# Attention over a graph: each head's row of shifts turned by VectorE and placed by four transfers, with the work around it moved

## The chip, the cores and the metric

The kernel runs on one core of a Trainium2 chip. The metric is the device time of one execution in microseconds (us); a comparison takes the median of several runs. The profile is of one execution. Its engines are TensorE (PE; PEld is its weight load), VectorE (DVE), ScalarE (ACT), GpSimd (POOL) and Sync (SP), whose queue issues all transfers here.

## The reference, cut to what matters

```python
h  = relu(layernorm(x))                              # 2048 x 256
hs = layer_norm(h, ln1);  ht = layer_norm(h_target, ln1)
q  = (ht @ Wq + bq) / sqrt(32); k = hs @ Wk + bk; v = hs @ Wv + bv     # 8 heads of 32
logits = where(adj != 0, q k^T, -1e30)               # 8 heads x 2048 targets x 2048 sources
ctx  = softmax(logits) @ v
ht = layer_norm(ht + ctx @ Wo + bo, ln2)
out = x + ht + gelu(ht @ W1) @ W2                    # W1 256 x 1024, W2 1024 x 256
```

`adj` is an int32 matrix of 2048 x 2048; `nodemask` masks nodes.

## The kernel before

**Tiling.** Targets go in four blocks (`NTB`) of 512. A block and a head make a unit `u` (32 in all, `k, r = divmod(u, 8)`: block `k`, place `r` in it). Each unit has 16 steps `s`, one per tile of 128 sources; `n = 16 u + s` numbers the tiles. Arithmetic is split into high and low 16-bit parts where precision asks for it.

**A softmax with a shift.** Exponentials need a shift per target, the negated maximum of its unmasked scores. It must be known before a unit's scores are made, so the scores are made twice. The "early" products (`early_scores`, 128 targets x 1024 sources, a "pair" `e`, 8 per unit) go into two PSUM buffers, where VectorE subtracts the mask and takes the maximum (`maxima`, L1123). These run ahead: in unit `u` at half-step `j` (two steps) the pair `8u + LEAD + j` is made, in `u0` two at a time at first (`pairs_at`). `RAMP = 8` pairs come ahead of the loop.

**How the shift reaches the scores.** ScalarE negates the four maxima columns (`negated`, L850) into column 96 of `shift` (128 x 4 x 97). TensorE multiplies the four slices by an identity (`shift_row`), which puts the shifts of the unit's 512 targets as row 96 into PSUM `aux`. ScalarE copies this row into row 96 of the queries `qT` (`row_out`, L855). Row 96 of `kT` holds ones, so the score product of 97 rows adds the shift. In a unit the negation stands at step 6, the products at step 8, the copy at step 9; the first score of the next unit is made at step 11, since scores run `AHEAD = 5` tiles ahead.

**A step.** TensorE: four mask products and one score product for tile `n + 5` (`scores`), half an early pair, now and then an auxiliary job, then the eight context products of tile `n` (`context`), which need the probabilities' low part. ScalarE: the exponential (L838). The low part, a subtraction of the bf16 high half, is VectorE's for the tiles in `DVE_LO` (L1131, four per unit) and GpSimd's for the others (L1333, twelve).

**Jobs between.** From block 1 on, units also hold what other blocks need: sums of the context's parts (`SUM_AT`, GpSimd), its normalising (`NORM_AT`, VectorE, L1150), its turning and output product (`CT_AT`, `WO_AT`), the next block's queries (`QT_AT`, `QP_AT`), the next masks (`MASK_DVE`, VectorE, L1111) and the loads of `adj` (`LOAD_AT`). Every order is written out by hand in each engine's queue. Sync's is in order too: in unit `r = 4` it issues twelve placements of the next block's queries (`place_q`), L350.

**The start.** After the projections, value products (`values(i)`, eight of them) leave PSUM as a high part (ScalarE, `high_values`) and a low one (VectorE, `low_values`, L1093). VectorE also adds up the features (`feature_sums`, L1098), from which TensorE makes a mean of the values (`mean_values`). Sync waits for `feat_done` before it loads W1 and W2 over the features, then places the last two groups of queries and keys, 30 placements, then loads `adj` for block 1.

**The tail.** Up products, gelu and down products by block. VectorE's `results(0)` come after the statistics of block 3 (`lead_stats`); the turning of the last context (`turn_context`) stands after the up products 5 and 6, the output rows (`out_row`) after 1 and 3.

## Time and profile before

| | |
|---|---|
| median of 3 runs | 711.27 us (708.77 to 711.74) |
| the profiled execution | 710.3 us, of which the span is 708.5 us |
| granted TensorE clock, mean | 0.995 of full speed |
| TensorE busy | 660.1 us |
| VectorE busy | 591.8 us |
| ScalarE busy | 455.1 us |
| GpSimd busy | 520.9 us |

A row in order of time gives start, duration, engine, line and operation, `out<-in`, shapes and a count; in brackets the idle time of the engine before it and what ended that. A busy time includes the pipeline's overlap for TensorE, so starts tell more than durations there.

### The profile page before, as it was taken

To read this page: it belongs to the slowest core of one execution; us is meant where nothing else is said; L and a number is where in the kernel's file an instruction comes from. 1 tells how busy PE (TensorE), PEld (TensorE's weight loads), DVE (VectorE), ACT (ScalarE), POOL (GpSimd) and SP (SyncE) were. 2 spreads that over 40 slices of the span, in tenths; PEclk is the share of its full clock that TensorE was granted. 3 is DMA by queue.
4 is the path that set the end of the run, shared out by engine and by line. 5 is a ranking of instruction groups with operands and counts; after the bars stand their busy time and mean duration, and the time that the engine had idled before them with its cause. 6 is when DMAs were issued, how large, how long until landed. Compare 5 with 4: busy or idle time off the path is not lost. (4 is left out here: it accounts for less than half of the span.)

```text
span 708.5 us, 20214 instructions
## 1 busy us (share of the span) xinstructions
PE 660.1 (93%) x8326; PEld 470.7 (66%) x8326; DVE 591.8 (84%) x972; ACT 455.1 (64%) x811; POOL 520.9 (74%) x495
## 2 busy tenths in 40 slices
PE   4996899999999999999999999999999899898998
PEld 4563566766776677667767766777677667456667
DVE  5996799989999989999999799989978897564661
ACT  4742566766776658677766686777666788756550
POOL 3620879889999966889999677999977777370430
PEclk9999999999999999999999999999999999999999
DMA  8735411113001020120001112021000000000001
GB/s 297 260 75 176 134 31 59 34 62 105 2 2 32 19 74 29 56 83 2 4 31 41 52 32 76 17 70 53 2 2 2 2 2 2 1 1 31 16 23 52
DMA packets 20795, 36.20 MB, mean 51 GB/s; under 512 B 2752, under 2 KB 13280, under 8 KB 20704
## 3 DMA queue, kind: packets, MB, share of 16 engines
q1 hardware_dynamic: 20704, 34.92, 15.8%
q8 instruction: 65, 1.06, 0.6%
q14 instruction: 26, 0.21, 0.1%
HBM read 26.49 MB, written 2.10 MB: 40 GB/s over the span
## 5 line engine op out<-in xcount | busy, mean ns | idle before, releaser
L1333 POOL TENSOR_TENSOR prob_lo<-prob 128x512 f16<-128x512 f32 x380 | 439.0, 1179 | 95.4 <-ACT prob L838 93.7
L838 ACT ACTIVATE prob<-score 128x512 f32<-128x512 f32 x512 | 305.0, 597 | 164.1 <-PE score L440 156.4
L440 PE MATMUL early<-kT,qT 96*128 96x512 f16 x512 | 192.2, 380 | 20.2 <-DVE half_max L1123 19.3
L440 PE MATMUL score<-nidentb,mask_nat 128*128 128x128 bf16 x2048 | 199.0, 220 | 2.9 <-ACT prob L838 1.6
L440 PE MATMUL score<-qT,kT 97*128 97x512 f16 x512 | 196.3, 383 | 0.0
L440 PEld LDWEIGHTS ctx<-v_sb,prob 128*128 128x128 bf16 x2048 | 159.1, 98 | 54.1 <-ACT raw L860 9.4
L440 PE MATMUL ctx<-v_sb,prob 128*128 128x65 f16 x2048 | 191.4, 193 | 0.6 <-POOL prob_lo L1333 0.5
L440 PE MATMUL ctx<-v_sb,prob_lo 128*128 128x65 f16 x2048 | 190.4, 193 | 0.0
L1123 DVE CUSTOM_DVE_ANT_0 early<-early,mask_nat,half_max 128x1024 f32<-128x1024 f32 x128 | 163.5, 1284 | 24.5 <-PE early L440 24.0
L1123 DVE CUSTOM_DVE_ANT_0 early<-early,mask_nat 128x1024 f32<-128x1024 f32 x128 | 156.8, 1228 | 23.2 <-PE early L440 21.2
L440 PEld LDWEIGHTS ctx<-v_sb,prob_lo 128*128 128x128 f16 x2048 | 142.7, 97 | 49.9 <-issue 4.0
L1131 DVE TENSOR_TENSOR prob_lo<-prob 128x512 f16<-128x512 f32 x132 | 132.9, 1008 | 4.1 <-ACT prob L838 4.0
L440 PEld LDWEIGHTS score<-nidentb,mask_nat 128*128 128x128 bf16 x2048 | 122.3, 98 | 6.8 <-ACT prob L838 3.7
L440 PEld LDWEIGHTS early<-kT,qT 96*128 96x128 f16 x512 | 50.3, 99 | 40.7 <-DVE half_max L1123 38.2
L1424 POOL TENSOR_TENSOR mask_nat<-mask_nat,tgt 128x256 f32<-128x256 f32 x16 | 15.3, 968 | 50.1 <-DVE mask_nat L1282 50.1
L440 PEld LDWEIGHTS score<-qT,kT 97*128 97x128 f16 x512 | 50.3, 98 | 0.0
L440 PE MATMUL early<-w_f,kT 128*128 128x256 f16 x384 | 42.8, 273 | 3.7 <-DVE adj_in L1292 3.7
L1268 DVE TENSOR_TENSOR kT<-qT,kT 128x512 f16<-128x512 f32 x32 | 27.0, 852 | 22.8 <-ACT kT L997 22.8
L440 PEld LDWEIGHTS early<-w_f,kT 128*128 128x128 f16 x384 | 37.4, 98 | 9.2 <-DVE adj_in L1292 4.2
L993 ACT ACTIVATE qT<-score 128x512 f32<-128x512 f32 x32 | 19.0, 593 | 25.3 <-PE score L440 22.0
L1123 DVE DVE_READ_ACCUMULATOR2_ANT half_max<- 128x1 f32 x256 | 35.2, 138 | 0.0
L1111 DVE TENSOR_SCALAR mask_nat<-adj_in 128x1024 bf16<-128x1024 int32 x26 | 29.9, 1153 | 0.0
(162 smaller groups left out, 597.2 us busy)
## 6 DMA issues: line engine op xcount, KB each, us to landing
adj_in<-in_adj SPq DMA_DIRECT2D x26, 512.0 KB, 3.9
qT<-q_stage SPq DMA_DIRECT2D x48, 64.0 KB, 2.0
kT<-mask_nat SPq DMA_DIRECT2D x48, 64.0 KB, 2.0
raw<-in_x SPq DMA_DIRECT2D x4, 512.0 KB, 5.6
tgt<-in_L_gnn_h_target SPq DMA_DIRECT2D x4, 512.0 KB, 11.4
prob<-in_adj SPq DMA_DIRECT2D x4, 512.0 KB, 10.2
nT<-in_L_gnn_W SPq DMA_DIRECT2D x2, 1024.0 KB, 6.8
mask_nat<-in_x SPq DMA_DIRECT2D x1, 2048.0 KB, 9.0
```

What stands on the lines that cost most here:

```text
L440: return nc.tensor.matmul(dst, w, m, start=start, stop=stop, **more)
L838: nc.scalar.activation(prob[:, n % SLOTS, :], score[n % 2][:, :], ACT.Exp).then_inc(exp_done, 1)
L993: nc.scalar.activation(gelu[:, f % 2, :], up[f % 2][:, :], ACT.Gelu_apprx_tanh).then_inc(gelu_ready, 1)
L1111: nc.vector.tensor_scalar(mask_half(k, i), adj_home(k, i), 0.0, BIG, ALU.is_equal, ALU.mult).then_inc(mask_dve, 1)
L1123: nc.vector.tensor_tensor_reduce(out=early[e % 2][:, :], in0=early[e % 2][:, :], in1=mask_nat[:, k % 2, t, half * HALF:(half + 1) * HALF], ...
L1131: nc.vector.tensor_tensor(prob_lo[:, n % SLOTS, :], prob[:, n % SLOTS, :], prob_hi(n % SLOTS), ALU.subtract).then_inc(lo_sem["dve"], 1)
L1268: nc.vector.tensor_tensor(g_lo[:, k % 2, f, :], gelu[:, f % 2, :], g_hi[:, k % 2, f, :], ALU.subtract).then_inc(g_lo_done, 1)
L1333: nc.gpsimd.tensor_tensor(prob_lo[:, n % SLOTS, :], prob[:, n % SLOTS, :], prob_hi(n % SLOTS), ALU.subtract).then_inc(lo_sem["pool"], 1)
L1424: nc.gpsimd.tensor_tensor(xin[:, n - 1, :], xin[:, n - 1, :], tgt[:, n - 1, :], ALU.add).then_inc(r_done, 1)
```

## The change

1. `negated` writes into columns 0 to 3 of `shift`, now 128 x 2 x 32. VectorE turns its 32 x 32 blocks (`turn_shifts`) into `shift_t`, where row `t` of each of the four blocks holds 32 shifts. Sync issues four transfers per unit (`place_shifts`), one per 128 targets, four pieces of 32 elements each, straight into row 96 of `qT`. The four products, the identity `ident16` and ScalarE's copy go.
2. The negation moves to step 3 (step 6 in `u0`), the turn stands on VectorE at half-step 2, ahead of its pair. `LEAD` becomes 16; `FILL = 4` more pairs come ahead of the loop, and `u0` has 12 pairs.
3. Moved: places of masks, adjacency loads (now before or after the unit's four transfers), sums, normalising, `CT_AT` and `WO_AT`. Every unit with `r = 5` gives VectorE three low parts in place of four, `u0` two in place of none.
4. At the start the low parts of value products 3 to 7 are GpSimd's, from an SBUF copy that ScalarE makes; the features are added up by six folds on GpSimd and one reduction on VectorE; the mean of the values follows the first five scores. `features(4)` and `high_parts(3)` move ahead on ScalarE, `target_stats(2)` behind on VectorE.
5. In the tail `turn_context` stands after the up products 5 and 7, `out_row` after 2 and 4, and the first two results between the statistics.

```diff
-LEAD = 14
+LEAD = 16
+FILL = 4
+V_DVE = 3
-SHIFT_STEP = 8
-CT_AT = {(2, 1): 0, (2, 4): 1}
-WO_AT = {(2, 11): 0, (3, 1): 1}
+SHIFT_AT, TURN_AT = 3, 2
+CT_AT = {(2, 6): 0, (2, 11): 1}
+WO_AT = {(2, 13): 0, (3, 1): 1}
-MASK_DVE = [(0, 6), (2, 1), (2, 4), (2, 7), (3, 7), (4, 3), (4, 7), (5, 3)]
-LOAD_AT = [0, 0, 0, 2, 2, 3, 4, 4]
-SUM_AT = [(0, 3), (0, 11), (1, 1), (1, 7)]
-NORM_AT = [(0, 5), (1, 1), (1, 3), (1, 5)]
+MASK_DVE = [(0, 6), (2, 4), (2, 6), (3, 2), (3, 7), (4, 3), (4, 7), (5, 3)]
+LOAD_AT = [(0, 0), (0, 0), (0, 1), (2, 1), (2, 1), (3, 1), (3, 1), (4, 1)]
+SUM_AT = [(0, 3), (0, 11), (1, 5), (2, 1)]
+NORM_AT = [(0, 5), (1, 1), (1, 5), (2, 2)]
-DVE_LO = [()] + [(2, 6, 10, 14)] * (UNITS - 3) + [tuple(range(1, STEPS, 2))] * 2
+DVE_LO = [(10, 14)] + [(4, 9, 14) if u % H == 5 else (2, 6, 10, 14) for u in range(1, UNITS - 2)] + [tuple(range(1, STEPS, 2))] * 2
...
+                def place_shifts(u):
+                    sp.wait_ge(shift_turned, u + 1)
+                    for t in range(TT):
+                        sp.dma_start(q_block(u // H)[SHIFT_ROW:SHIFT_ROW + 1, u % H, t * P:(t + 1) * P],
+                                     shift_t[t::HD, u % 2, :]).then_inc(shift_in[u % 2], 16)
...
                 sp.wait_ge(v_ready, NT // 2)
                 sp.wait_ge(feat_done, 1)
+                place_shifts(0)
...
-                            if LOAD_AT[i] == r:
+                            if LOAD_AT[i] == (r, 0):
+                                load_adj(k + 1, i)
+                    if u + 1 < UNITS:
+                        place_shifts(u + 1)
+                    if k + 1 < NTB:
+                        for i in range(PAIRS):
+                            if LOAD_AT[i] == (r, 1):
                                 load_adj(k + 1, i)
...
-                        pe.wait_ge(aux_done, AUX["shift", u] + 1)
+                        pe.wait_ge(shift_in[u % 2], TT * 16 * (u // 2 + 1))
...
-                def shift_row(u):
-                    pe.wait_ge(shift_ready, u + 1)
...
-                    for t in range(TT):
-                        last = mm(aux[0:SHIFT_ROW + 1, t * P:(t + 1) * P], shift[:, t, :], ident16[:, :], True, True)
-                    last.then_inc(aux_ready, 1)
...
-                for e in range(TT, RAMP):
+                for e in range(TT, RAMP + FILL):
                     for i in range(2):
                         early_scores(e, i)
-                    if e == RAMP - 2:
-                        mean_values()
-                shift_row(0)
                 for n in range(AHEAD):
                     scores(n)
+                mean_values()
...
-                    nc.scalar.activation(shift[:, :, SHIFT_ROW], half_max[:, u % 2, 1, :], ACT.Copy, scale=-1.0).then_inc(
-                        shift_ready, 1)
-
-                def row_out(u):
-                    job_here("shift", u)
-                    nc.scalar.activation(q_block(u // H)[SHIFT_ROW:SHIFT_ROW + 1, u % H, :], aux[SHIFT_ROW:SHIFT_ROW + 1, :],
-                                         ACT.Copy).then_inc(aux_done, 1)
+                    nc.scalar.activation(shift[:, u % 2, 0:TT], half_max[:, u % 2, 1, :], ACT.Copy, scale=-1.0).then_inc(shift_ready, 1)
...
-                        job = aux_job(u, s + 2)
-                        if job == ("shift", u + 1):
+                        if s == SHIFT_AT + 3 * (u == 0) and u + 1 < UNITS:
                             negated(u + 1)
...
+                def turn_shifts(u):
+                    dve.wait_ge(shift_ready, u + 1)
+                    if u > 1:
+                        dve.wait_ge(shift_in[u % 2], TT * 16 * (u // 2))
+                    nc.vector.transpose(shift_t[:, u % 2, :], shift[:, u % 2, :]).then_inc(shift_turned, 1)
...
                 for e in range(TT, RAMP):
                     maxima(e)
+                turn_shifts(0)
+                maxima(RAMP)
+                dve.wait_ge(folded, 6)
+                nc.vector.tensor_reduce(feat_all[:, :], fold[:, 0, :, 0:TB // 8], AX, ALU.add).then_inc(feat_done, 1)
+                for e in range(RAMP + 1, RAMP + FILL):
+                    maxima(e)
...
+                        if j == TURN_AT and u + 1 < UNITS:
+                            turn_shifts(u + 1)
                         for e in pairs_at(u, j):
                             maxima(e)
...
+                def fold_features(i):
+                    if i < 2:
+                        pool.wait_ge(nT_masked, DC * (2 * i + 2))
...
+                        dst, a, b = fold[:, i, :, :], nT[:, 2 * i, :, :], nT[:, 2 * i + 1, :, :]
...
+                fold_features(0)
+                for i in range(V_DVE, NT // 2):
+                    low_values(i)
+                    fold_features(i - V_DVE + 1)
...
                 for t in range(TT):
+                    if t % 2 == 0:
+                        result(0, t // 2)
                     lead_stats(NTB - 1, t, t == TT - 1)
                 lead_scale(NTB - 1, lead_width(NTB - 1))
-                results(0)
+                for t in range(2, TT):
+                    result(0, t)
```

## Rows read from the trace of the kernel before

**Rows 1.** The page: busy time, share of the span and instructions of each engine.

```profile
PE 660.1 (93%) x8326; PEld 470.7 (66%) x8326; DVE 591.8 (84%) x972; ACT 455.1 (64%) x811; POOL 520.9 (74%) x495
```

**Rows 2.** Windows of u1, u5, u7, u9 (start:end): length, each engine's busy time, clock, DMA.

```profile
93.05:109.46 16.41, 15.08 (x233) 10.88 (x231) 14.75 (x23) 10.62 (x20) 13.86 (x14) 1.00 0.11 33
160.02:177.05 17.03, 15.57 (x233) 10.71 (x231) 17.03 (x23) 11.12 (x21) 15.74 (x14) 1.00 0.38 110
191.96:206.86 14.90, 14.90 (x233) 10.91 (x231) 13.52 (x21) 11.02 (x22) 14.90 (x14) 1.00 0.01 2
221.83:239.01 17.18, 15.48 (x233) 10.78 (x231) 17.18 (x25) 10.63 (x21) 17.18 (x17) 1.00 0.11 32
```

**Rows 3.** TensorE in u7, in order of time: mask products of three steps.

```profile
198.08 0.39 PE L440 MATMUL score<-nidentb,mask_nat 128*128 128x128 bf16 x4
...
198.98 0.39 PE L440 MATMUL score<-nidentb,mask_nat 128*128 128x128 bf16 x4
...
200.11 0.39 PE L440 MATMUL score<-nidentb,mask_nat 128*128 128x128 bf16 x4
```

**Rows 4.** Groups of instructions: busy us, mean ns of one, idle before.

```profile
L1131 DVE TENSOR_TENSOR prob_lo<-prob 128x512 f16<-128x512 f32 x132 | 132.9, 1008 | 4.1 <-ACT prob L838 4.0
...
L855 ACT ACTIVATE qT<-aux 1x512 f16<-1x512 f32 x32 | 18.9, 589 | 1.3 <-PE aux L440 0.5
...
L1150 DVE TENSOR_TENSOR q_stage<-raw,rden 128x256 f32<-128x256 f32 x16 | 13.2, 824 | 0.0
...
L440 PE MATMUL aux<-ident,shift 128*97 128x128 f16 x128 | 12.4, 218 | 2.0 <-ACT shift L850 2.0
```

**Rows 5.** The same view: VectorE's small operations.

```profile
L1170 DVE TENSOR_TENSOR col_l<-col_l,node_f 128x4 f32<-128x4 f32 x4 | 2.9, 723 | 0.1
...
L1169 DVE RECIPROCAL col_l<-col_l 128x4 f32<-128x4 f32 (+1 forms) x4 | 0.7, 180 | 0.4 <-ACT col_l L878 0.4
```

**Rows 6.** Sync's queue in order of time: issues of transfers, in three stretches.

```profile
2.32 0.33 SPq L371 DMA_DIRECT2D vec_r<-in_L_gnn_ln_scale  x1
...
4.44 0.25 SPq L371 DMA_DIRECT2D vec_r<-in_L_gnn_ln_bias  x1
...
60.57 0.90 SPq L409 DMA_DIRECT2D nT<-in_L_gnn_W  x2
...
81.90 1.08 SPq L345 DMA_DIRECT2D adj_in<-in_adj  x2
...
296.29 8.25 SPq L350 DMA_DIRECT2D qT<-q_stage  x12
```

**Rows 7.** Issues of transfers by tile: KB each, median us from issue to landing.

```profile
adj_in<-in_adj SPq DMA_DIRECT2D x26, 512.0 KB, 3.9
...
kT<-mask_nat SPq DMA_DIRECT2D x48, 64.0 KB, 2.0
...
kT<-ones SPq DMA_DIRECT2D x1, 32.0 KB, 10.4
```

**Rows 8.** The start in order of time: GpSimd's last masking, TensorE's products.

```profile
40.09 2.63 POOL L1357 TENSOR_TENSOR nT<-nT,qT 128x512 f32<-128x512 f32 x2 [3.58 <-ACT nT L784]
...
56.20 1.99 PE L440 MATMUL ctx<-cT,nT 128*128 128x256 f32 x8 [1.96 <-DVE v_sb L1093]
58.55 1.99 PE L440 MATMUL aux<-cT,nT 128*128 128x256 f32 x8 [0.35 <-DVE v_sb L1093]
...
68.18 0.48 PE L440 MATMUL score<-nidentb,mask_nat 128*128 128x128 bf16 x4 [0.68 <-ACT qT L855]
```

**Rows 9.** VectorE in u0 in order of time: the first maxima of two half-steps.

```profile
80.41 1.29 DVE L1123 CUSTOM_DVE_ANT_0 early<-early,mask_nat,half_max 128x1024 f32<-128x1024 f32 x1 [0.32 <-PE early L440]
...
83.28 1.29 DVE L1123 CUSTOM_DVE_ANT_0 early<-early,mask_nat,half_max 128x1024 f32<-128x1024 f32 x1 [0.32 <-PE early L440]
```

**Rows 10.** TensorE in the tail in order of time: its two longest waits.

```profile
617.30 0.63 PE L590 MATMUL aux<-ident,q_stage 128*128 128x128 f32 x4 [2.66 <-ACT cT L869]
...
646.38 5.41 PE L440 MATMUL early<-w_f,kT 128*128 128x256 f16 x48 [2.96 <-DVE adj_in L1292]
```

More of the change, by code:

```diff
@@ L81, in aux_job @@
     k, r = divmod(u, H)
-    if s == SHIFT_STEP + (u == 0):
-        return ("shift", u + 1) if u + 1 < UNITS else None
     if k + 1 < NTB and (r, s) in QT_AT:
@@ L102, in aux_numbers @@
 def aux_numbers():
-    jobs = [("shift", 0)] + [aux_job(u, s) for u in range(UNITS) for s in range(STEPS) if aux_job(u, s)]
+    jobs = [aux_job(u, s) for u in range(UNITS) for s in range(STEPS) if aux_job(u, s)]
     jobs += [("cT", NTB - 1, c) for c in range(DC)] + [("wo", NTB - 1, i) for i in range(TT // 2)]
@@ L116, in pairs_at @@
     if u == 0:
-        first = RAMP + (2 * j if j < 6 else j + 6)
-        return range(first, first + (2 if j < 6 else 1))
+        first = RAMP + FILL + (2 * j if j < 4 else j + 4)
+        return range(first, first + (2 if j < 4 else 1))
     first = u * PAIRS + LEAD + j
@@ L191, in gnn_kernel @@
         mean_v = sb("mean_v", [P, H, VS], F16)
-        shift = sb("shift", [P, TT, SHIFT_ROW + 1], F16)
+        shift = sb("shift", [P, 2, HD], F16)
+        shift_t = sb("shift_t", [P, 2, HD], F16)
         half_max = sb("half_max", [P, 2, 2, TT], F32)
@@ L310, in value_bank, with value_read @@
                 return early[1][:, i * TB:(i + 1) * TB]
-            return (score if i < 4 else (ctx, aux))[i % 2][:, :]
+            return ((ctx, aux) if i in (4, 5) else score)[i % 2][:, :]
+        def value_read(eng, i):
+            if i < V_DVE:
+                eng.wait_ge(v_lo, i + 1)
+            else:
+                eng.wait_ge(v_out, i - V_DVE + 1)
         def raw_of(k):
@@ L529, in scores @@
                     if n < 2:
[L531 removed]
+                        value_read(pe, n + 6)
                     else:
@@ L1209, in _ @@
                 low_values(0)
-                for k in range(1, 3):
-                    target_stats(k)
+                target_stats(1)
                 low_parts(2)
+                target_stats(2)
                 low_values(1)
@@ L1283, in shifted_rows, with result @@
                                                        in1=xin[:, n, :], op0=ALU.mult, op1=ALU.add).then_inc(t1_done, 1)
+                def result(k, t):
+                    n = k * TT + t
+                    dve.wait_ge(r_done, n + 1)
+                    dve.wait_ge(down_ready, n + 1)
+                    if n >= 4:
+                        dve.wait_ge(stored[n % 4], n // 4 * 16)
+                    nc.vector.scalar_tensor_tensor(out=yout[:, n % 4, :], in0=row[n % 2], scalar=node_f[:, n:n + 1],
+                                                   in1=xin[:, n, :], op0=ALU.mult, op1=ALU.add).then_inc(y_done, 1)
                 def results(k):
                     for t in range(TT):
[L1287 to L1293 removed]
+                        result(k, t)
                 denominators(NTB - 1)
@@ L1358, in drop_sources, with low_values @@
                                                 ALU.mult).then_inc(nT_masked, 1)
+                def fold_features(i):
+                    if i < 2:
+                        pool.wait_ge(nT_masked, DC * (2 * i + 2))
+                        if i == 0:
+                            pool.wait_ge(tp_ready, DC * len(GROUPS))
+                        dst, a, b = fold[:, i, :, :], nT[:, 2 * i, :, :], nT[:, 2 * i + 1, :, :]
+                    else:
+                        pool.wait_ge(folded, i)
+                        half = TB >> (i - 2)
+                        dst, a, b = fold[:, 0, :, 0:half], fold[:, 0, :, 0:half], fold[:, 0, :, half:2 * half] if i > 2 else fold[:, 1, :, :]
+                    nc.gpsimd.tensor_tensor(dst, a, b, ALU.add).then_inc(folded, 1)
+                def low_values(i):
+                    pool.wait_ge(v_hi, i + 1)
+                    full = v_full[:, i % 2, :].rearrange("p (t h d) -> p t h d", t=2, h=H)
+                    tiles = slice(2 * i, 2 * i + 2)
+                    nc.gpsimd.tensor_tensor(v_sb[:, tiles, :, HD:2 * HD], full, v_sb[:, tiles, :, 0:HD], ALU.subtract).then_inc(v_lo_pool, 1)
                 def context_sum(k, t):
@@ L1372, in _ @@
                 nc.gpsimd.memset(dead_w[:, :], DEAD_W).then_inc(made, 1)
-                for m in (ident32, identb, nidentb, ident16):
+                for m in (ident32, identb, nidentb):
                     last = nc.gpsimd.memset(m[:, :], 0.0)
                 link(last)
-                for m, one in ((identb, 1.0), (ident32, 1.0), (nidentb, -1.0), (ident16, 1.0)):
+                for m, one in ((identb, 1.0), (ident32, 1.0), (nidentb, -1.0)):
                     last = nc.gpsimd.affine_select(out=m[:, :], in_=m[:, :], compare_op=ALU.not_equal, fill=one, base=0,
```

78 lines of the change are left out of this document (29 added, 49 removed).

## The prediction

> **What bounds the kernel now.** The order of reading: the page's engine row, the windows by head unit, the order in time of TensorE inside one unit, the waits of the slow units, then the start and the tail. A "unit" is one head of one block of 512 targets; there are 32, u0 to u31, of 16 steps each. TensorE is busy 93% of the span and VectorE 84% [rows 1], but the mean hides two kinds of unit. In u7 TensorE has no idle time in 14.90 us, while VectorE is busy 13.52: TensorE bounds it. In u5 VectorE is busy in all of the 17.03 us and TensorE in 15.57; in u9 VectorE and GpSimd are busy in all of the 17.18 us and TensorE in 15.48 [rows 2]. u13 and u21 look like u5; u17 and u25 like u9. ScalarE is never above 0.75 of such a window. So a TensorE instruction taken out is worth its time in most units, in these six only a VectorE instruction is.
>
> **The products that go.** In u7 the starts of two mask products one step apart are 198.08 and 198.98: a step is 0.90 us. The step that also holds the four shift products is 198.98 to 200.11, 1.13 us [rows 3]. The mean of 218 ns of each product [rows 4] is mostly pipeline overlap; what leaves the queue is 0.225 us for four. It counts in the units that TensorE bounds: u2 to u30 without the six, 23 units, **-5.2 us**. ScalarE's copy of the row, 589 ns [rows 4], I count at nothing: ScalarE is busy 11.02 of 14.90 us in u7 [rows 2], and that idle time hides it; without that cover it would be worth 0.6 us a unit.
>
> **The turn and the transfers that come.** No row shows VectorE turning a block. It moves 32 columns of 128 rows. The nearest rows are of 128x4: a reciprocal at 180 ns, and a two-input operation at 723 ns [rows 5], whose like can be as short when nothing holds it. I take 0.2 us, near the first, because it too has one input; the ends are 0.1 and 0.7. In u7 VectorE has 1.4 us to spare, so even 0.7 is hidden there; in the six it is on the path.
> The four transfers: the smallest issues of the trace, eight of two rows each, start 0.30 us apart (2.32 to 4.44, seven steps); an issue of 32 rows takes 0.6 to 0.7 (12 in 8.25 us) [rows 6]. I take 0.30 each, since a shift transfer has four tiny pieces: 1.2 us in all, at most 2.7. From issue to landing the placements take 2.0 us; the ones, a one-partition transfer issued behind loads, took 10.4 [rows 7]. Is that early enough? The maxima now run two pairs further ahead (LEAD 16), so those of unit u+1 are done when unit u begins. ScalarE negates after its fourth exponential of unit u; VectorE turns after its second pair there. In u7 the step of 198.98 is step 8, so the unit starts at 198.98 - 8 x 0.905 = 191.7; the second pair's products end with step 3, at 195.3, its maximum 1.3 us later [rows 9], at 196.6. Plus 0.2, 1.2 and 2.0 makes 200.0. The first score of the next unit is issued at step 11, 191.7 + 11 x 0.905 = 201.7. So 1.7 us of slack: hidden, **0**. Everything behind that score on TensorE (context products, and through them ScalarE, GpSimd) would stop if it were late.
> Sync's queue is in order. At the end of r=4 it issues 12 placements of queries in 8.25 us [rows 6], for u12 until 304.54, and the new transfers of u13 come behind: 305.8, landing 307.8, while step 11 of u13 is at about 307.3. That is 0.3 us late on the mean of u5, u13, u21. They in turn lose one of four residual subtractions on VectorE (1008 ns [rows 4]; with it GpSimd has 15.74 + 1.2 us of work in u5 [rows 2], some 0.7 more than the unit would last, which the five steps by which scores run ahead absorb) and gain the turn: -1.0 + 0.2 + 0.3, three times: **-1.5 us**. u9, u17, u25 lose one normalising product of VectorE (824 ns [rows 4]) and a sum on GpSimd to r=2, where TensorE bounds: -0.82 + 0.2, three times: **-1.9 us**. The other moved masks and adjacency loads stay within the units' VectorE cover and come before the loads of the same step: 0; without cover each would cost about what a subtraction does, 1.0 us.
> u30 no longer has the last two pairs (early products): four products of 512 columns, each as many columns as the four shift products together, 0.22 us: **-0.9 us**.
>
> **The start.** At 56.20 and 58.55 TensorE waits 1.96 and 0.35 us for VectorE's residuals of v [rows 8]. These go to GpSimd behind a ScalarE copy, and the feature sums too, so the remaining four pairs of u0 begin at about 58 instead of 58.55 + 1.8 = 60.4, and are done near 63. But the shifts of u0 are placed only after Sync's wait for feat_done, and that now hangs on GpSimd: from 43 on, six folds and five residuals. Two instructions of 512 elements took 2.63 us [rows 8], so 1.2 to 1.3 each. The first fold is free; the first residual waits for the fourth value product and two ScalarE copies, until about 50. From there five residuals (6 us) and folds of 1024, 1024, 512, 256 and 128 elements (7 us), with a tenth for collisions and 0.3 for the reduction: I get 64.8 for feat_done, 66.0 for the last issue, 68.0 for landing. The first score was at 68.18 [rows 8]: nothing is gained, and the mean products, now behind the first five scores, put 0.9 us on TensorE less what they cover: context starts **+0.4 us**. (Four more pairs are hidden in this gap.)
> u0 has 12 pairs in place of 14; two pairs take VectorE 2.87 us (80.41 to 83.28), 0.32 of it waiting [rows 9]. Two steps with one pair cost 1.8, so this is -2.1. But the turn for u1 stands before VectorE's fifth pair, and waits for a negation placed behind ScalarE's exponential of step 6, which needs TensorE's score of step 6: VectorE idles about 2.5 us. Then the row for u1 is late: Sync starts its 30 placements about 5.4 us later than before (feat_done 64.8 and 1.2 of issues against 60.57), so the two loads issued at 81.90 [rows 6] go out at 87.3, and the transfers last at 89.6, behind 1 MB that needs until about 92 (such a load lands in 3.9 us [rows 7], two in about 5). Step 11 of u0 would be at about 89.6: 2.5 us of stall. From this VectorE catches up, and u1's 1.3 us of TensorE idle (16.41 against 15.08 busy [rows 2]) go. Sum -2.1 + 2.5 + 2.5 - 1.3, and 1.4, two thirds of 2 x 1.0, for the two subtractions that u0 now gives VectorE: **+3.0 us**.
>
> **The tail.** At 646.38 TensorE idles 2.96 us for a result row held behind VectorE's statistics [rows 10]; results 0 and 1 now go between them: -2.9. At 617.30 it idles 2.66 us for ScalarE's cT [rows 10]; with an up product in front of it 1.2 of that is filled. **-4.1 us**.
>
> **Sum:** -5.2 - 1.5 - 1.9 - 0.9 + 0.4 + 3.0 - 4.1 = -10.2 us. The profiled execution took 710.3 us (708.5 of span, 1.8 around it), so 700.1; the median of the three runs is 1.0 above that one: **701 us**.
>
> **A rule to weigh.** The row first: the two-input operation on 128x4 takes 723 ns on the mean for 4 columns [rows 5], beside a GpSimd that is nearly always busy. The Trainium skill (SBUF — State Buffer, "SBUF: two separate sides") says why: VectorE operations with two SBUF inputs and GpSimd's share one pair of ports, whoever starts first has it for the whole instruction. By that rule moving folds and residuals to GpSimd can hold the masks of the start by one fold each (an estimate from that page and the rows: three times 1 us, which would make it 704), while the maxima, which read PSUM and one SBUF operand, go on. The sum above does without it.
>
> **Rivals.**
> 1. The row is late in every unit. For: the slack is 1.7 us, and no row shows so small a transfer between partitions. Against: placements of 64 KB land in 2.0. It costs from the point where turn, issues and landing exceed 201.7 - 196.6 = 5.1 us; with 0.62 us per issue and a landing of 3.9, it is 6.6: 1.5 late, 31 times, less the 10: 748; with half of that excess 724. Slower.
> 2. The start costs more: the transfers for u1 land as late after issue as the 10.4 us row, or the folds on GpSimd are held up (the rule's locks): about 6 us more, 707.
> 3. The turn costs 0.7 us: six units lose 0.5 each, 704.
> 4. The start costs nothing: VectorE does not idle at the turn, and the loads do not hold the row: 695.
>
> **Chances and range.** Forecast 0.54 (own range 697 to 704.5); rival 1 0.08; rival 2 0.15, about half of it still over 0.5% faster; rival 3 0.10; rival 4 0.13. 0.5% is 3.6 us, about what three runs of this kernel can tell from nothing. Faster 0.54 + 0.13 + 0.10 + 0.07 = 0.84; same 0.08; slower 0.08. Range 693 to 709: rival 4 with the turn at 0.1 below, rival 2 with its bound above; rival 1 stays outside.
>
> **What would show it.** Steps of u7 all at 0.90 and its window at 14.7; u5 near 16.1 and u9 near 16.6; a TensorE wait before the first score of u1 of some 2.5 us, named a DMA wait, and VectorE idle 2.5 us before the turn for u1; feat_done's reduction near 64.5; no TensorE idle of 3 us in the tail. I am wrong if TensorE waits for a transfer in unit after unit, or if the first score comes after 71.

## The result, and the profile after

| | median | runs | ratio to before, with its 95% interval |
|---|---|---|---|
| before | 710.1 us (708.77 to 711.74) | 6 | |
| changed | 715.0 us (714.19 to 717.78) | 6 | 1.0071 [1.0049, 1.0093] |

The changed kernel is 0.7% slower, 4.9 us. The forecast was 701.0 with a range of 693 to 709, so the sign was wrong too. The profiled execution took 714.19 us, its span is 712.4; before, 710.3 and 708.5. These 3.9 us of span are placed first. The page of the changed kernel, busy times:

```profile
PE 656.2 (92%) x8198; PEld 463.4 (65%) x8198; DVE 595.2 (84%) x993; ACT 438.6 (62%) x784; POOL 538.3 (76%) x506
```

TensorE has less to do (656.2 against 660.1 [rows 1]) and yet more time passes. Windows of the changed kernel, the same view as [rows 2]: u0 from its first score on, u1, u5, u7, u9 and u10; length, busy time of PE, PEld, DVE, ACT, POOL, then clock, DMA share, GB/s.

```profile
71.95:103.28 31.33, 24.33 (x266) 15.87 (x267) 18.22 (x33) 13.01 (x24) 17.12 (x17) 0.87 0.57 165
103.28:119.36 16.08, 14.75 (x229) 10.58 (x227) 14.76 (x23) 10.03 (x19) 14.10 (x14) 1.00 0.10 34
169.96:186.29 16.33, 14.89 (x229) 10.60 (x227) 15.82 (x24) 10.42 (x20) 15.71 (x14) 1.00 0.20 49
200.86:215.43 14.57, 14.57 (x229) 10.63 (x227) 14.21 (x23) 10.44 (x21) 14.57 (x14) 1.00 0.22 75
230.46:247.52 17.06, 14.93 (x229) 10.66 (x227) 17.06 (x27) 10.04 (x20) 16.91 (x16) 1.00 0.10 33
247.52:268.50 20.98, 19.12 (x255) 13.93 (x252) 18.66 (x34) 11.18 (x23) 17.70 (x18) 1.00 0.16 51
```

u7 lost 0.33 us, u5 0.70, u9 0.12. Before, u0 lasted 24.87 us from its first score (68.18 to 93.05) at a mean clock of 0.93; now it lasts 31.33 at 0.87. u10 lasts 20.98 us against 19.32. The whole, stretch by stretch (a unit ends where ScalarE copies its context):

| stretch | predicted | measured |
|---|---|---|
| up to the first score | +0.4 | +3.8 |
| u0 and u1 | +3.0 | +6.5 - 0.3 |
| the products, 22 units and u30's part | -5.2 | 19 of them -1.7; u10, u18, u26 +1.7, +1.6, +1.5 |
| u5, u13, u21 | -1.5 | -0.70, -0.85, -0.91 |
| u9, u17, u25 | -1.9 | -0.12, -0.13, -0.38 |
| u30's early products | -0.9 | -1.4, with its part of the products |
| tail (end of u30 to the end) | -4.1 | -4.6 |
| sum | -10.2 | +3.9 |

Of the 14 us between the sums, two places carry 11: the start (9.9 against 3.4) and the units r = 2 (4.7 against nothing). The rest is mostly the products.

**The start.** VectorE of the changed kernel, in order of time:

```profile
38.72 3.04 DVE L1117 TENSOR_SCALAR mask_nat<-adj_in 128x1024 bf16<-128x1024 int32 x2
41.68 3.43 DVE L1117 TENSOR_SCALAR mask_nat<-prob 128x1024 bf16<-128x1024 int32 x2
45.03 0.74 DVE L1096 SCALAR_TENSOR_TENSOR mask_nat<-ctx,cols,mask_nat 128x512 f16<-128x512 f32 x1
```

GpSimd in the same stretch:

```profile
38.10 2.71 POOL L1375 TENSOR_TENSOR nT<-nT,qT 128x512 f32<-128x512 f32 x2 [1.69 <-ACT nT L798]
...
41.17 2.78 POOL L1389 TENSOR_TENSOR raw<-nT 128x1024 f32<-128x1024 f32 x1
```

and TensorE:

```profile
45.92 3.62 PE L466 MATMUL ctx<-nT,cT 128*128 128x512 f32 x4 [2.73 <-DVE mask_nat L1096]
```

Before, the same two pairs of masks:

```profile
38.10 1.28 DVE L1111 TENSOR_SCALAR mask_nat<-adj_in 128x1024 bf16<-128x1024 int32 x2
39.30 1.29 DVE L1111 TENSOR_SCALAR mask_nat<-prob 128x1024 bf16<-128x1024 int32 x2
```

Now the first pair lies beside GpSimd's last masking and takes 3.04, and the second beside the first fold (L1389, whose result the third fold, at 60.18, is the first to read) and takes 3.43. The first mask of the second pair by itself, seen in a narrower window:

```profile
41.68 2.83 DVE L1117 TENSOR_SCALAR mask_nat<-prob 128x1024 bf16<-128x1024 int32 x1
```

It starts 0.5 us into the fold and ends at 44.51, 0.56 us after the fold's end (43.95); such a mask takes 0.69 us in the kernel before. The residuals behind the masks (L1096) are 3.7 us late, TensorE waits 2.73 us for them, and the key products that follow take 3.62 us (1.96 in experiments 1 and 4, below): the window 45.85 to 49.26 has a granted clock of 0.50, the lower of the two levels (1.2 GHz).

Sync's queue, in order of time:

```profile
68.64 2.23 SPq L369 DMA_DIRECT2D qT<-shift_t  x4
70.91 0.95 SPq L429 DMA_DIRECT2D nT<-in_L_gnn_W  x2
71.92 1.86 SPq L362 DMA_DIRECT2D qT<-q_stage  x3
73.82 8.46 SPq L362 DMA_DIRECT2D kT<-mask_nat  x12
82.32 1.92 SPq L362 DMA_DIRECT2D qT<-q_stage  x3
84.28 8.21 SPq L362 DMA_DIRECT2D kT<-mask_nat  x12
92.54 1.08 SPq L357 DMA_DIRECT2D adj_in<-in_adj  x2
93.66 2.22 SPq L369 DMA_DIRECT2D qT<-shift_t  x4
```

Four shift transfers take 2.2 us to issue (each 492 ns, 0.58 us from one start to the next), where 1.2 was predicted. The two adjacency loads go out at 92.54, where the prediction had 87.3, and the four transfers for u1 from 93.66 on. TensorE in u0 waits for both the turn and the row:

```profile
88.57 0.60 PE L466 MATMUL early<-kT,qT 96*128 96x512 f16 x2 [2.26 <-DVE half_max L1129]
...
98.43 0.40 PE L466 MATMUL score<-nidentb,mask_nat 128*128 128x128 bf16 x4 [2.81 <-DMA qT<-shift_t]
```

The turn at the same place on VectorE:

```profile
87.07 0.21 DVE L1140 STREAM_TRANSPOSE shift_t<-shift 128x32 f16<-128x32 f16 x1 [2.80 <-ACT shift L870]
```

The turn takes 0.21 us, as taken, and idles 2.80 us for the negation, as foreseen (2.5).

**Windows at the lower clock.** These three stretches of the changed kernel are found in its clock record (the column behind the busy times):

```profile
45.85:49.26 3.41, 3.34 (x4) 1.51 (x5) 2.92 (x5) 0.00 (x0) 0.00 (x0) 0.50 0.23 57
66.33:76.57 10.24, 7.73 (x32) 3.40 (x33) 5.68 (x12) 2.70 (x6) 4.64 (x6) 0.50 0.42 131
90.23:93.64 3.41, 3.41 (x33) 2.29 (x30) 2.50 (x5) 1.19 (x2) 1.04 (x1) 0.50 0.35 84
```

Together 17.1 us; the kernel before has two stretches of 3.4 us, one at its first scores and one in the tail (experiment 8). The first of the three comes at the end of the wait of 2.73 us, the third 1.7 us after that of 2.26. Ahead of the second TensorE waited 1.1, 0.6 and 0.6 us before three early pairs. The longest wait, 2.81 us at 98.43, was followed by none.

A wait doesn't settle whether a stretch follows. Experiment 4 has the start of the changed kernel unchanged, and the same wait:

```profile
45.85 1.96 PE L466 MATMUL ctx<-nT,cT 128*128 128x512 f32 x4 [2.67 <-DVE mask_nat L1096]
```

Here the four products take 1.96 us at full clock, no stretch is near, and the first score comes at 70.24, 1.7 us before the changed kernel's. So of the +3.8 at the first score, 2.1 are the late masks and 1.7 the half clock behind them.

Executions of one kernel differ mostly in their time at half clock. Of the kernel before, those at a mean clock of 0.998 have spans of 706.8 to 707.3 us, those at 0.995 708.4 to 708.8, those at 0.990 710.9 to 711.6 and those at 0.986 714.2 to 714.3. The changed kernel's three at 0.988 (712.4 to 712.7) lie between the last two: its loss comes together with more time at half clock, and at a like clock it is no slower than the kernel before. How much of that time waits hide, no run separates. So 1.7 us between two single profiles can be one stretch more or less.

**r = 2.** TensorE in u10, whose window is above:

```profile
255.56 0.66 PE L608 MATMUL aux<-ident,q_stage 128*128 128x128 f32 x4 [1.20 <-DVE q_stage L1163]
```

The turned context (`CT_AT`, step 6) waits for the normalising (L1163), which the change moved to the same unit; in u26 the same wait is 0.92 us, in u18 only 0.22. u10 and u18 also have one of 0.61 us for a low part of GpSimd. I had counted the units r = 2 as bound by TensorE and the moved work as free there.

### The profile page after: what moved, and what is told of

Read it like the earlier page. It is cut to its first block and busy times, and to the rows that moved or that the text cites. A ratio compares the mean times of both kernels' runs of the same rounds, so it can differ in the third digit from the quotient of the medians.

```text
span 712.4 us, 20092 instructions
## 1 busy us (share of the span) xinstructions
PE 656.2 (92%) x8198; PEld 463.4 (65%) x8198; DVE 595.2 (84%) x993; ACT 438.6 (62%) x784; POOL 538.3 (76%) x506
## 5 line engine op out<-in xcount | busy, mean ns | idle before, releaser
L1144 DVE TENSOR_TENSOR prob_lo<-prob 128x512 f16<-128x512 f32 x130 | 137.4, 1060 | 1.1 <-ACT prob L858 0.7
L1117 DVE TENSOR_SCALAR mask_nat<-adj_in 128x1024 bf16<-128x1024 int32 x26 | 27.2, 1050 | 0.0
```

The source lines that it names most:

```text
L1117: nc.vector.tensor_scalar(mask_half(k, i), adj_home(k, i), 0.0, BIG, ALU.is_equal, ALU.mult).then_inc(mask_dve, 1)
L1144: nc.vector.tensor_tensor(prob_lo[:, n % SLOTS, :], prob[:, n % SLOTS, :], prob_hi(n % SLOTS), ALU.subtract).then_inc(lo_sem["dve"], 1)
```

## The experiments

Each ratio is to runs of the kernel before on the same chip (medians 710.6). "Changed" is the kernel of the change; its median was 715.0, beside 710.1 for the kernel before.

**1. The first fold waits for the masks.** Changed, with one more wait on GpSimd:

```diff
@@ fold_features
                         if i == 0:
                             pool.wait_ge(tp_ready, DC * len(GROUPS))
+                            pool.wait_ge(mask_dve, TT)
```

> The changed kernel, with one wait more: GpSimd's first fold waits until VectorE has made its four first masks. Theory (collision): in the changed kernel these four masks take 6.4 us instead of 2.4, because the fold and they hold the same ports; TensorE then waits 2.7 us and runs 3.4 us at the half clock. With the wait the masks take 2.4 to 3.5 us, TensorE reaches the fourth key projection at about 43.2 instead of 45.9, there is no half-clock stretch there, the first score starts about 4 us earlier (68 instead of 72), and the time falls by 4 to 5 us, to about 710.5. Rival (the start is held by Sync and the transfers alone, the collision is absorbed): under 1 us of change.

Measured: 712.5 us (10 runs), ratio 1.0021 [0.9997, 1.0046], 2.5 less than changed. VectorE of this kernel:

```profile
38.70 3.05 DVE L1117 TENSOR_SCALAR mask_nat<-adj_in 128x1024 bf16<-128x1024 int32 x2
41.67 1.28 DVE L1117 TENSOR_SCALAR mask_nat<-prob 128x1024 bf16<-128x1024 int32 x2
42.87 0.74 DVE L1096 SCALAR_TENSOR_TENSOR mask_nat<-ctx,cols,mask_nat 128x512 f16<-128x512 f32 x1
```

The second pair is back at 1.28 us, the first still lies beside GpSimd's masking. TensorE in the same place:

```profile
43.75 1.96 PE L466 MATMUL ctx<-nT,cT 128*128 128x512 f32 x4 [0.58 <-DVE mask_nat L1096]
```

Its wait is 0.58 instead of 2.73, the clock stays up, and the first score is issued at 68.13 instead of 71.95. So one fold in the wrong place, with the stretch at half clock behind it, explains the whole +3.8 at the first score. The expectation of 4 to 5 us in all was nearly twice too high. The 3.9 us are still there at the end of u1; 2.0 go between u2 and u30, in u5, u13 and u21 (rows up to 0.4 us later) and in u17 and u18, where this execution has a stretch at half clock that the changed kernel's has not.

**2. The row of u1 ahead of the last placements.** Changed; Sync issues the transfers of u1 before the fourth head pair's placements:

```diff
                 for g in range(2, TT):
+                    if g == 3:
+                        place_shifts(1)
                     place_q(0, range(g, g + 1))
...
-                    if u + 1 < UNITS:
+                    if 0 < u < UNITS - 1:
                         place_shifts(u + 1)
```

> The changed kernel, with Sync's four transfers for u1 moved ahead of the last 15 placements and of the two loads of the next block. Theory (the row queues behind 30 placements and 1 MB): the wait of 2.8 us before u1's first score is gone and the time falls by 2.5 to 3 us, to about 712.3. Rival (the wait only hides another, the late turn on VectorE): under 1 us. Rival 2 (the 15 placements, now later, hold the first mask of block 1): no change or slower by up to 3 us.

Measured: 718.7 us, ratio 1.0125 [1.0101, 1.0148]. No TensorE wait for the row of u1 is left and u0 ends at 100.37 instead of 103.28, but u1 lasts 20.83 us instead of 16.08. A row of VectorE of this kernel:

```profile
104.53 0.69 DVE L1119 TENSOR_SCALAR mask_nat<-adj_in 128x1024 bf16<-128x1024 int32 x1 [3.99 <-DMA adj_in<-in_adj]
```

The wait went from the row to the adjacency of block 1, which now stands behind it in Sync's queue, and grew: TensorE waits 4.56 us there.

**3. u0's turn one pair later.** Changed, with `if j == TURN_AT + (u == 0)` for VectorE's turn.

> The changed kernel, with VectorE's turn for u1 one half-step later in u0 (after the fifth and sixth pair and not before them). Theory: VectorE's idle time of 2.8 us before the turn and TensorE's wait of 2.3 us behind it go, and the half-clock stretch at 90 us too, but the row still queues in Sync's queue, which is free only at 93.7: the wait before u1's first score grows by what is saved, and the time changes by less than 1 us. Rival (the turn's idle time is on the path): 2 to 4 us faster.

Measured: 716.8 us, ratio 1.0096 [1.0074, 1.0119]. VectorE's idle time at the turn is gone, and TensorE's wait for the row grew from 2.81 to 6.15 us; u0 ends at 105.17. The 1.8 us more than changed aren't clear of the scatter, since two of the changed kernel's six runs lie at 716.8 and 717.8. While Sync is the bottleneck, filling VectorE's gap gives nothing.

**4. The moved jobs back.** Changed, with the tables as in the kernel before:

```diff
-CT_AT = {(2, 6): 0, (2, 11): 1}
-WO_AT = {(2, 13): 0, (3, 1): 1}
-MASK_DVE = [(0, 6), (2, 4), (2, 6), (3, 2), (3, 7), (4, 3), (4, 7), (5, 3)]
-LOAD_AT = [(0, 0), (0, 0), (0, 1), (2, 1), (2, 1), (3, 1), (3, 1), (4, 1)]
-SUM_AT = [(0, 3), (0, 11), (1, 5), (2, 1)]
-NORM_AT = [(0, 5), (1, 1), (1, 5), (2, 2)]
+CT_AT = {(2, 1): 0, (2, 4): 1}
+WO_AT = {(2, 11): 0, (3, 1): 1}
+MASK_DVE = [(0, 6), (2, 1), (2, 4), (2, 7), (3, 7), (4, 3), (4, 7), (5, 3)]
+LOAD_AT = [(0, 0), (0, 0), (0, 1), (2, 1), (2, 1), (3, 0), (4, 0), (4, 1)]
+SUM_AT = [(0, 3), (0, 11), (1, 1), (1, 7)]
+NORM_AT = [(0, 5), (1, 1), (1, 3), (1, 5)]
```

> The changed kernel, with the places of the context's turning and output product, of masks, loads, sums and normalising inside the units as in the kernel before. Theory (the moved jobs cost what the removed products save): the units u10, u18, u26 (21.0, 20.0, 20.4 us in the changed kernel) fall by 1.5 to 2 us each and u11, u19 by 0.4, the time falls by 4 to 6 us, to about 710. Rival (VectorE's turn and the lead of the maxima cost it, wherever the jobs stand): these units stay within 0.5 us and the time within 1 us.

Measured: 710.4 us (10 runs), ratio 1.0003 [0.9988, 1.0018], 4.6 less than changed. Windows of u9 and u10 in this kernel:

```profile
227.72:245.54 17.82, 15.25 (x231) 10.53 (x228) 17.82 (x26) 10.01 (x19) 17.82 (x18) 1.00 0.10 31
245.54:264.79 19.25, 18.38 (x255) 14.01 (x252) 18.24 (x34) 11.15 (x22) 16.16 (x16) 1.00 0.17 57
```

The moved jobs relieve u9 by 0.76 us (17.06 against 17.82) and load u10 by 1.73 and u11 by 0.79. With them back, u10, u18 and u26 together are 0.5 under the kernel before, and the 19 units that the table counts apart 3.7 under it. (This profile is of the fastest of the ten executions.)

**5. Another order of Sync's start.** Changed; all 30 placements and both rows go ahead of the wait for the feature sums:

```diff
-                sp.wait_ge(v_ready, NT // 2)
-                sp.wait_ge(feat_done, 1)
                 place_shifts(0)
-                for i, (dst, w) in enumerate(((w1, W1), (w2, W2))):
...
                 for g in range(2, TT):
...
+                place_shifts(1)
+                sp.wait_ge(v_ready, NT // 2)
+                sp.wait_ge(feat_done, 1)
+                for i, (dst, w) in enumerate(((w1, W1), (w2, W2))):
...
-                    if u + 1 < UNITS:
+                    if 0 < u < UNITS - 1:
                         place_shifts(u + 1)
```

> The changed kernel with another order in Sync's queue at the start and nothing else: after the four shift transfers of u0 come the placements of the last two head pairs, then the shift transfers of u1, and only behind them the wait for the feature sums and the two weight loads; in the changed kernel the shifts of u0 waited for the feature sums and those of u1 stood behind 24 placements, four weight and adjacency loads. Theory (the row for u1 waits in Sync's queue, and the row for u0 for the feature sums): first score at 70.8 instead of 71.95, the DMA wait of 2.8 us before u1's first score gone, u0 ends near 99.5, and the kernel takes about 711. Rival (row_first showed it: what is moved ahead delays the next thing, now the weight loads or block 1's adjacency, and TensorE waits for VectorE's mask instead): u1 ends no earlier than in the changed kernel, 715.

Measured: 717.5 us, ratio 1.0086 [1.0056, 1.0117]. The rival held. (Against the 715.0 of changed the 2.5 us more are not clear of the scatter: the intervals overlap.) The first score comes at 70.49 and u0 ends at 99.42, both as the theory said, but u1 lasts 21.07 us: TensorE waits 4.21 us for the maxima and these for block 1's adjacency, as in experiment 2. Order alone can't mend a queue with more in it than time.

**6. Order, fold and jobs together.** Experiments 5, 1 and 4 in one kernel.

> The Sync order of sp_order, the first fold on GpSimd held until VectorE's four masks are done (fold_waits), and the places of the moved work in r=1 to r=4 as before (jobs_back), together. Theory: the three repairs lie in different stretches and add up: the order about -4, the fold -2.5, the places -4.5, from 715, makes 704. Rival: the start's repairs overlap, since each removes the lateness of the same first score and of the same row for u1, and all that they give together is what the larger gives: 707 or more.

Measured: 704.6 us, ratio 0.9915 [0.9885, 0.9945]. It was the size that the theory gave, though not by its terms: the order, counted at -4, gave nothing alone, and with the other two (-2.5 and -4.6) it gives the 3.3 that are left of the 10.4. The first score is at 66.97, u0 ends at 95.19, and u1 still lasts 20.51 us. VectorE of this kernel:

```profile
98.75 0.95 DVE L1118 TENSOR_SCALAR mask_nat<-adj_in 128x1024 bf16<-128x1024 int32 x1 [3.39 <-DMA adj_in<-in_adj]
```

**7. Only the shift path on the kernel before**, with the order of experiment 5 and u0's turn for u1 one pair later: turn, transfers, `LEAD = 16`, `FILL = 4`; sums, value parts, jobs and tail untouched.

> The kernel before with only the shift row changed: VectorE's turn and four transfers instead of the products and the copy, with 16 pairs of lead, and the Sync order of sp_order. The feature sums, the value residuals, the places of masks, loads, sums and normalisings, and the tail stay as in the kernel before. Theory (the shift path itself gains in the units that TensorE bounds, 0.33 us each in 23 units, 0.9 for u30, and costs 2 to 3 us in the start): 705. Rival (it is the shift path that costs; the moved work is innocent): not faster than before, 710 or more.

Measured: 719.4 us, ratio 1.0118 [1.0083, 1.0154]. The theory's 705 was wrong by 14 us. Sync begins the placements at 70.85 (the turn of u0 stands ahead of them), against 61.5 before, and u0 ends at 103.10, 10 us late; from u1's end to u30's it is 4.0 us shorter than before. The profile is of the slowest of the four (722.0), and 2.9 of its loss lie in the tail, where nothing was changed: it has stretches at half clock by the two long waits there, 10.2 us in all, against 3.4 in the kernel before.

**8. Only the tail's moves on the kernel before:**

```diff
-                    if f in (5, 6):
-                        turn_context(NTB - 1, f - 5)
+                    if f in (5, 7):
+                        turn_context(NTB - 1, f // 2 - 2)
...
-                    if f in (1, 3):
+                    if f in (2, 4):
...
                 for t in range(TT):
+                    if t % 2 == 0:
+                        result(0, t // 2)
                     lead_stats(NTB - 1, t, t == TT - 1)
...
```

> The kernel before with only the tail's moves: the second turned context one place later, the output rows one place later, the first two results of block 0 between VectorE's row statistics. Theory: TensorE's idle times of 2.66 and 2.96 us near 617 and 646 go, the kernel is 4 to 5 us faster than before, 706, and nothing changes ahead of the tail. Rival: the tail gains only because the changed kernel comes to it without the half-clock stretch, so that the moves alone give less than 2 us.

Measured: 705.5 us, ratio 0.9928 [0.9904, 0.9952], 5.1 less than before. Both long waits of [rows 10] are gone. What is left in TensorE's tail:

```profile
616.41 1.47 PE L440 MATMUL score<-nTq,w_f 128*128 128x512 f16 x6 [1.43 <-ACT qT L993]
619.00 4.06 PE L440 MATMUL score<-qT,w_f 128*128 128x512 f16 x18 [0.69 <-DVE qT L1176]
628.80 1.13 PE L440 MATMUL aux<-wo,cT 128*128 128x256 f32 x4 [0.54 <-ACT tgt L873]
```

Gone as well is a stretch at half clock that followed the wait at 617.30 in the kernel before; a window of that kernel:

```profile
617.90:621.30 3.40, 3.40 (x10) 1.22 (x8) 1.30 (x3) 1.73 (x4) 0.00 (x0) 0.50 0.00 0
```

But the stretch doesn't hang on the wait alone. Experiment 11 keeps the old tail with both waits, and runs on at full clock behind the first:

```profile
615.59 0.63 PE L601 MATMUL aux<-ident,q_stage 128*128 128x128 f32 x4 [2.66 <-ACT cT L871]
615.59:619.00 3.41, 3.41 (x18) 1.83 (x19) 2.06 (x5) 2.84 (x6) 0.00 (x0) 1.00 0.00 0
```

Its tail is 1.7 us shorter than the kernel before's by that alone. Of the 5.1 us here some 3.4 are thus the moves; executions of both kernels at a mean clock of 0.998 say the same (703.7 us of span against 706.8 to 707.3).

**9. Sync's idle time filled.** Experiment 6, and Sync, which had nothing to issue from 54.5 to 63.5, issues there two loads and nine placements that stood behind the turn:

```diff
+                for i in range(2):
+                    load_adj(1, i)
+                place_q(0, range(2, 3))
+                for c in (0, 1):
+                    place_k(c, range(2, 3))
                 place_shifts(0)
...
```

> sp_fold_jobs (704.6) with nothing but Sync's idle time ahead of the first shift transfers filled: the two adjacency loads of block 1, the three query and six of the twelve key placements of the third head pair are issued there, 9 us of the 54 that stood behind it. Theory (Sync's queue sets the end of u0 and u1): the mask of block 1 no longer waits for its load, TensorE's wait of 4.2 us in u1 goes, u1 lasts 16.5 instead of 20.5, and the kernel takes 700.5. Rival (the wait is replaced by one for placements or for bandwidth, since the same bytes and issues are still to be moved): u1 19 us or more, 703 or more.

Measured: 702.6 us, ratio 0.9876 [0.9840, 0.9912]. Sync's queue of this kernel:

```profile
54.62 1.14 SPq L357 DMA_DIRECT2D adj_in<-in_adj  x2
55.80 1.79 SPq L362 DMA_DIRECT2D qT<-q_stage  x3
57.63 3.77 SPq L362 DMA_DIRECT2D kT<-mask_nat  x6
63.40 2.65 SPq L369 DMA_DIRECT2D qT<-shift_t  x4
```

VectorE no longer idles for block 1's mask and u1 lasts 16.02 us, so the mechanism was right, though 700.5 was expected and the median gained only 2.0. The gain in span is 3.0 us: 4.5 in u1, less 0.65 up to the end of u0 and 0.8 in the units after u1 (in u5 TensorE waits 1.48 us for its row, 1.00 in experiment 6).

**10. The same, with u0's turn one pair later**, the edit of experiment 3.

> sp_early with u0's turn for u1 one pair of VectorE later. In turn_later, where the row waited in Sync's queue, this gave nothing (the kernel took 2 us more). Theory: with Sync's queue free, VectorE's idle time at that turn (2.3 us of TensorE wait behind it) is on the path now, and goes: 1 to 2 us less than sp_early. Rival: the row for u1 becomes late instead, no gain or a loss.

Measured: 697.9 us (697.69 to 698.25, 6 runs), ratio 0.9809 [0.9773, 0.9844]. What gave nothing in experiment 3 gives 4.6 us here, more than expected. u0 from its first score on, in experiment 9:

```profile
67.18:95.84 28.66, 24.39 (x266) 15.83 (x267) 18.30 (x31) 13.00 (x23) 17.81 (x17) 0.86 0.41 123
85.59:89.00 3.41, 3.41 (x33) 2.31 (x30) 2.45 (x4) 1.19 (x2) 1.08 (x2) 0.50 0.79 277
```

and in experiment 10:

```profile
67.09:91.62 24.53, 22.67 (x266) 14.86 (x267) 18.13 (x31) 13.00 (x23) 18.24 (x17) 0.90 0.45 128
```

u0 is 4.13 us shorter: 2.26 of TensorE's wait, and the 3.41 us at half clock that followed it, worth half of that, 1.7. Another 1.3 us of span come in u5, u13 and u21, whose rows are less late.

**11. Experiment 7 with Sync's idle time filled.**

> shift_only (719.4: the kernel before with only the shift row changed) with Sync's idle time ahead of the first shift transfers filled as in sp_early. In shift_only the 30 placements and the weight and adjacency loads all stood behind the turn of u0 (from 68.6 us on, against 60.6 in the kernel before), and VectorE and TensorE waited for them: 4.6 us for the row of u1, 2.2 us for the mask of block 1. Theory (what the shift path costs is its place in Sync's queue): 8 to 10 us come back, 710. Rival (the cost lies in VectorE's order in the start, the first score at 72 instead of 68.2): less than 3 us come back, 717.

Measured: 707.3 us (10 runs), ratio 0.9945 [0.9918, 0.9972], 12.1 less than experiment 7. The theory held: u0 ends at 96.28 and u1 lasts 15.17 us, 10.4 us between them in the profiles. (The profiles differ by 4.6 more in the tail, which is the half clock alone.) By the medians the shift path with this order of Sync is 3.3 us faster than the kernel before, with its first score still at 72.8. The kernel before was never given that order, so how much of the 3.3 is the path and how much the order isn't shown.

**12. The turned context two steps later.** Changed, with `CT_AT = {(2, 8): 0, (2, 11): 1}`.

> The changed kernel with only the first turned context of a block moved from step 6 to step 8 of r=2, two steps behind the wait of 1.2 us that u10 shows for the moved normalising. Theory (the moved normalising at r=2 is late for the turned context, and TensorE waits for it in u10, u18, u26): u10 19.8 instead of 20.98, u18 and u26 alike, 3 to 3.5 us less than the changed kernel, 711.5 to 712. Rival (the unit is bound by the work that came into it, VectorE's and GpSimd's, and the wait only shows where): u10 stays above 20.6, 714 or more.

Measured: 712.5 us (10 runs), ratio 1.0024 [0.9996, 1.0052], 2.5 less than changed. u10 lasts 20.01, u18 19.54, u26 19.23 (20.98, 19.99, 20.36 in the changed kernel): 2.55 us together of the 4.7 that these units had lost. So over half of the cost goes when the turned context comes later, most of it where the wait was longest (u26 1.13, u10 0.97; u18, with a wait of 0.22, 0.45). The rest stays with the further work of those units, VectorE being busy 19.87 of u10's 20.01 us and the wait of 0.60 for GpSimd's low part still there:

```profile
247.16:267.17 20.01, 19.23 (x261) 14.16 (x257) 19.87 (x36) 11.18 (x22) 17.54 (x18) 1.00 0.09 28
```

## Why the prediction was wrong, by its own steps

**Context starts +0.4 (measured +3.8).** The step that failed is "the first fold is free": it made the masks late by enough to hold TensorE 2.73 us, and 1.7 of half clock came behind that. I had priced exactly this collision in the paragraph on the rule, as three times 1 us and 704, and left it out of the sum. The Trainium skill (SBUF — State Buffer, "SBUF: two separate sides") says that VectorE in its fast two-port modes, or with two SBUF inputs, and GpSimd lock each other out for a whole instruction, the second kind only against a GpSimd operation that reads SBUF. The masks have one SBUF input, so for them it can only be the fast mode, which no row here names; the prediction told the rule for two inputs alone. In its effect the trace agrees: a mask of 0.69 us that started into a fold ended only after it, 2.83 us later, and two took 1.28 again once the fold was held back (experiment 1). I had looked for the cost in the residuals and folds late in the start; it was in the four masks. feat_done came near 68.6, not 64.8: the first residual on GpSimd started at 54.79, not at 50. In experiment 5 the row of u0 no longer waited for it and the first score came 1.5 us earlier (70.49).

**u0 and u1 +3.0 (measured +6.1).** Turn stall 2.26, predicted 2.5. Row late 2.81, predicted 2.5: nearly the same number, but only by luck, because both sides of it moved: TensorE reached that score at 95.6 instead of 89.6, and the row was there at 98.4 instead of 92. Experiment 10 shows u0 without these stalls at 24.53 us. 24.53 + 2.26 + 2.81 + 1.7 for the stretch at half clock is 31.3, the 31.33 measured. The term that was missing is the 1.7: in all eight kernels here that have this wait, a stretch at half clock starts within 1.9 us of its end. What the -2.1 for fewer pairs and the +1.4 for two subtractions came to one by one wasn't told apart; 24.53 against 24.87 is their sum with what the clock took. u1's -1.3 was -0.33: TensorE's idle time there stayed.

**Issues 0.30 us apart (measured 0.58).** The size of "four tiny pieces" was taken from the nearest row; the bound given (0.6 to 0.7) held. In the start, where Sync has a backlog, the miss counts 1.0 us for each row. In the steady units it cost nothing. In u6 the turn starts at 190.95, the four issues end at 193.28, and TensorE waits for no row. Rival 1 is refuted, as is rival 3: the turn takes 197 ns on the mean of 32. In u5, u13 and u21 the row was late by 1.0, 0.9 and 0.8 us, not 0.3: its four issues come right behind the twelve placements, as foreseen, and take 2.2 us there (178.20 to 180.41 for the row awaited in u5, whose score follows at 181.46), 1.0 more than in the sum.

**The products, -5.2 for 23 units.** The sign was right, the size too small per unit and counted for too many units. A unit that TensorE bounds lost 0.33 us, not 0.225. In the kernel before, TensorE's steps in u7 are 0.90 us but for the one of 1.13 and, two steps behind it, one of 1.00 (mask products at 201.01 and 202.01). At that place ScalarE has the copy of the row ahead of an exponential:

```profile
201.37 0.59 ACT L855 ACTIVATE qT<-aux 1x512 f16<-1x512 f32 x1
201.98 1.28 ACT L838 ACTIVATE prob<-score 128x512 f32<-128x512 f32 x2
```

Both long steps are gone after the change. That the copy made the second one is read from this order, not shown by a run. But u8, u12, u16, u20, u28 and u29 gained nothing. In u8 and u16 GpSimd is busy in all of the window (15.03 of 15.03 us in u8), in u12 and u28 TensorE waits 1.0 us for VectorE's maxima. The 19 units gave 3.7 us with the jobs back.

**Moved work "0 in r = 2" (measured +4.7 in u10, u18, u26).** This is the largest failed step besides the start. I checked VectorE's cover in these units but not who waits for the moved result. Experiment 4 brings 5.3 us back in these three units at the price of 2.3 in u9, u17 and u25; experiment 12 shows that over half hangs on where the turned context stands. **u9, u17, u25 -1.9** gave -0.6, because the shift path alone makes them 0.64, 0.64 and 0.39 us longer (experiments 4 and 11). The turn adds 0.2 us to VectorE, which bounds them; the other 0.4 is open.

**u5, u13, u21 -1.5, u30 -0.9 and the tail -4.1** were right in mechanism: -2.5, -1.4 with its products, -4.6. In the tail the near hit is partly luck: both waits went, but of the 4.6 to 5.1 us some 1.7 are a stretch at half clock in the kernel before's profile that experiment 11 lacks with the same waits.

**Rival 2** (the start costs more, 707) is nearest to what came. Of its two causes the GpSimd locks were there, but on the masks; the late row was there too, by Sync's backlog and not by a slow landing. It was given 0.15. Even without the jobs at r = 2 the kernel takes 710 (experiment 4), not 707. The mark given for "wrong", a first score after 71, was met: 71.95.

What stays open: why TensorE's clock falls for 10.24 us at the first scores wherever the sums and value parts are moved (but for 6.83 in experiment 5), for 6.83 in experiments 7 and 11, and for 3.4 in the kernel before; no experiment changed only the early pairs' spacing. Why the same wait in the start or the tail has a stretch behind it in one run and none in another. What Sync's better order would give the kernel before. And which of the moved work makes u11 and u19 0.8 us longer.

## What to carry to other kernels

Price an in-order queue by its whole backlog: four transfers of 256 bytes cost 2.2 us of Sync each time, and behind an event they delay everything later, so fill the queue's idle time ahead of that event first; reordering only moved the wait. Repairs on a shared path don't add up: the later turn gave nothing while the queue was late and 4.6 us once it wasn't, so try each again after the bottleneck has moved. Compare the clock of two profiles before explaining a difference of a microsecond or two. When a job moves to a unit with time to spare, look for its consumer, not only for its engine's idle time; and don't leave a collision that you have priced out of the sum.

## What the runs showed of the hardware

- Two VectorE masks from int32 took 1.28 us alone and 3.04 to 3.43 beside a GpSimd operation with two SBUF inputs, though they have only one SBUF input. One that started 0.5 us into such an operation of 2.78 us ended 0.56 us after it.
- A transfer of four pieces of 64 bytes took 492 ns to issue (median of 128), against 591 ns for a placement of 64 KB (median of 96): 256 times the bytes, a fifth more time. The eight small vector loads at the start took 231 to 325 ns each.
- Behind TensorE's wait of 2.26 us in u0 came a stretch at the 1.2 GHz level in eight of eight kernels; behind 2.73 us at the first masks in the changed kernel but not behind 2.67 in experiment 4; behind 2.66 in the tail in the kernel before and experiment 7 but not in experiment 11. Where TensorE is busy throughout a stretch of 3.4 us, it costs 1.7 us more than the wait (experiments 4 and 10).
- VectorE's turn of 32 columns by 128 rows took 0.20 us.
